# A conditioned LoRA kernel: tile 1 of x loaded behind W and transposed by VectorE, and the rounded part of M multiplied in front of its remainder

## The reference, cut to what matters

```python
# x (64, 32, 512): 64 samples of 32 rows; W0 (16, 32, 32); W (512, 512); A (5, 512, 32); Bw (512, 32)
x = x + einsum('bct,bcd->bdt', x, W0[cond])           # mix: each sample's 32 rows by its own 32x32 matrix
x = x + einsum('bsi,oi->bso', x, W)                    # base, the same for all samples
      + 0.5 * einsum('bsr,or->bso', einsum('bsi,bir->bsr', x, A[label]), Bw)
```

## Time and profile before

| | us |
|---|---|
| median of 3 runs | 75.79 (75.51, 75.79, 79.14) |
| the profiled execution, its own time | 74.88 |
| its span in the trace | 73.1 |
| PE busy | 69.3 |
| DVE busy | 41.7 |
| ACT busy | 34.9 |
| POOL busy | 32.2 |

### The profile page before, as it was taken

How to read it: one execution, slowest core, us unless ns; L and a number is a source line. 1 busy time by engine, 2 the same in 40 slices (tenths; PEclk the granted TensorE clock), 3 DMA queues, 4 the chain that set the end, 5 groups by cost and what they waited for, 6 DMA issues and landing times.

```text
span 73.1 us, 2439 instructions
## 1 busy us (share of the span) xinstructions
PE 69.3 (95%) x1006; PEld 55.7 (76%) x1006; DVE 41.7 (57%) x64; ACT 34.9 (48%) x83; POOL 32.2 (44%) x75
## 2 busy tenths in 40 slices
PE   4999999999999999999999999999999999999950
PEld 3788999987786768888687588888876788858930
DVE  4018769999489799919972669439016190213220
ACT  1536667699033974729702452834915538004100
POOL 4652678699980047878932058867000100000000
PEclk9999999999999999999999999999999999999999
DMA  0989999345397650048965000059910000599694
GB/s 7 328 259 372 226 238 205 63 134 151 101 211 263 182 127 13 9 95 196 283 174 158 9 4 17 19 137 181 247 36 9 0 0 0 117 192 264 186 241 158
DMA packets 11727, 10.25 MB, mean 140 GB/s; under 512 B 1092, under 2 KB 9028, under 8 KB 11716
## 3 DMA queue, kind: packets, MB, share of 16 engines
q1 hardware_dynamic: 11200, 9.83, 53.2%
q0 software_dynamic: 512, 0.26, 1.9%
q10 hardware_dynamic: 4, 0.00, 0.0%
HBM read 5.90 MB, written 4.19 MB: 138 GB/s over the span
## 4 chain that ended last, share of the span: by engine, by line
PE 95%; DVE 1%; issue 0%
PE p_u L642 18%; PE p_u L643 17%; PE p_u L644 17%; PE p_low L624 7%; PE p_y L653 5%; PE p_u L648 4%; PE p_low L709 4%; PE p_y L686 4%; PE p_fold L633 3%; PE p_y L642 3%; PE p_y L644 3%; PE p_y L643 3%; PE p_y L678 1%; PE p_low L695 1%; PE p_fold L695 1%; PE p_low L644 1%
## 5 line engine op out<-in xcount | busy, mean ns | idle before, releaser
L642 PE MATMUL p_u<-m_hi,xt_hi 128*128 128x512 f32 (+2 forms) x66 | 24.1, 364 | 0.0
L643 PE MATMUL p_u<-m_lo,xt_hi 128*128 128x512 f32 (+2 forms) x66 | 23.3, 354 | 0.0
L644 PE MATMUL p_u<-m_hi,xt_lo 128*128 128x512 f32 (+2 forms) x66 | 23.3, 354 | 0.0
L291 POOL DMA_INDIRECT w_sel<-in_L_cond_weights,w_row x16 | 16.9, 1057 | 12.3 <-PE p_y L653 8.0
L642 PEld LDWEIGHTS p_u<-m_hi,xt_hi 128*128 128x128 f32 x66 | 12.5, 189 | 2.2 <-issue 0.6
L644 PEld LDWEIGHTS p_u<-m_hi,xt_lo 128*128 128x128 f32 x66 | 12.5, 189 | 1.8
L643 PEld LDWEIGHTS p_u<-m_lo,xt_hi 128*128 128x128 f32 x66 | 12.5, 189 | 1.6
L469 DVE STREAM_TRANSPOSE xt<-x_sb 128x512 f32<-128x512 f32 x12 | 13.0, 1105 | 0.1
L498 DVE COPY u_sb<-p_u 128x512 f32<-128x512 f32 x6 | 4.2, 692 | 12.4 <-PE p_u L648 10.1
L370 ACT ACTIVATE xt_hi<-xt 128x512 fp32r<-128x512 f32 x12 | 6.9, 627 | 7.3 <-PE p_u L648 5.1
L492 DVE TENSOR_TENSOR xt_lo<-xt,xt_hi 128x512 fp32r<-128x512 f32 x12 | 8.4, 732 | 0.2
(11 more groups left out here) (80 smaller groups left out, 80.2 us busy)
## 6 DMA issues: line engine op xcount, KB each, us to landing
x_sb<-in_x SPq DMA_DIRECT2D x24, 128.0 KB
out<-y_sb SPq DMA_DIRECT2D x12, 256.0 KB
w_sb<-in_L_cond_W SPq DMA_DIRECT2D x4, 256.0 KB, 4.1
x_rows<-in_x SPq DMA_DIRECT2D x2, 256.0 KB, 3.5
x_rows<-in_x SPq DMA_DIRECT2D x1, 512.0 KB, 5.0
out<-y_two SPq DMA_DIRECT2D x4, 128.0 KB
a_sb<-in_L_cond_lora_A SPq DMA_DIRECT2D x1, 320.0 KB
w_sel<-in_L_cond_weights,w_row POOLq DMA_INDIRECT x16, 4.0
```

What stands on the lines that cost most here:

```text
L291: nc.gpsimd.indirect_dma_start(out=w0_sel[:, t, :], out_offset=None, in_=W0_rows, in_offset=bass.IndirectOffsetOnAxis(ap=w0_row[:, t:t + 1 ...
L642: mm(to, xt_hi[:, slot, c, rows], m_hi[:, c, cols], start=(c == 0 and first), stop=False)
L643: mm(to, xt_hi[:, slot, c, rows], m_lo[:, c, cols], start=False, stop=False)
L644: mm(to, xt_lo[:, slot, c, rows], m_hi[:, c, cols], start=False, stop=False)
```

## The change

SP loads all four blocks of W one behind the other. Tile 1 comes behind them, not as rows but as the second half of pair 0 in the layout of the pairs (four DMAs of 64 KB), in slot 0 of `x_sb`. DVE transposes it between the remainders of the third and the fourth block of M; ACT rounds it behind its fourth `split_m`; DVE subtracts. The second `transpose_rows`, `split_rows` and `keep_rows` are gone. Pair 2 uses the same slot, so its load waits for that transpose (`s_x1_t`). On PE the products of tile 0 with `m_hi` (eight matmuls a half) stand in front of those with `m_lo` (four a half), each half in 256 columns, and tile 1 is one `main_tile` of 512 columns.

```diff
             sp.dma_start(x_rows[:, 0], x_tile[0]).then_inc(s_rows_in[0], 16)
-            for o in W_ORDER[:2]:
+            for o in W_ORDER:
                 sp.dma_start(w_sb[:, o], W[P * o:P * (o + 1), :]).then_inc(s_w_in[o], 16)
-            sp.dma_start(x_rows[:, 1], x_tile[1]).then_inc(s_rows_in[1], 16)
-            for o in W_ORDER[2:]:
-                sp.dma_start(w_sb[:, o], W[P * o:P * (o + 1), :]).then_inc(s_w_in[o], 16)
+            for q in range(Q):
+                sp.dma_start(x_sb[R * q:R * (q + 1), 0, 1], x_pair[0, q][:, BT:2 * BT]).then_inc(s_x1_in, 16)
             sp.dma_start(bw_sb[:].rearrange("p o r -> p (o r)"), Bw_cols).then_inc(s_bw_in, 16)
             load(1, 1)
             sp.dma_start(a_sb[:].rearrange("p (l n) -> p l n", l=NL), A_cols).then_inc(s_a_in, 16)
+            sp.wait_ge(s_x1_t, 1)
             load(2, 0)
...
             split_m(1)
-            split_rows(1, p_fold)
             split_m(2)
             split_m(3)
+            act.wait_ge(s_x1_t, 1)
+            nc.scalar.activation(xt_hi[:, 0, :, P:2 * P], xt[:, 0, 1], COPY).then_inc(s_xhi, 1)
             keep_rows(0, p_low)
...
-            keep_rows(1, p_fold)
...
             split_m(1)
-            split_rows(1, p_fold)
             split_m(2)
+            dve.wait_ge(s_x1_in, 16 * Q)
+            nc.vector.transpose(xt[:, 0, 1].rearrange("p c (b s) -> p c b s", s=S),
+                                x_sb[:, 0, 1].rearrange("p b (i c) -> p c b i", c=C)).then_inc(s_x1_t, 1)
             split_m(3)
+            dve.wait_ge(s_x1_t, 1)
+            dve.wait_ge(s_xhi, 2)
+            nc.vector.tensor_tensor(xt_lo[:, 0, :, P:2 * P], xt[:, 0, 1], xt_hi[:, 0, :, P:2 * P].bitcast(F32),
+                                    ALU.subtract).then_inc(s_xlo, 1)
...
+            def main_rounded(bank, u, cols, first):
...
+                for c in range(C):
+                    mm(bank[:, cols], xt_hi[:, 0, c, rows], m_hi[:, c, cols], start=(c == 0 and first), stop=False)
+                for c in range(C):
+                    mm(bank[:, cols], xt_lo[:, 0, c, rows], m_hi[:, c, cols], start=False, stop=False)
+
+            def main_remainder(bank, u, cols):
...
+                for c in range(C):
+                    mm(bank[:, cols], xt_hi[:, 0, c, rows], m_lo[:, c, cols], start=False, stop=False)
...
             transpose_w(1)
-            transpose_rows(1, p_fold)
...
+            transpose_w(2)
+
+            pe.wait_ge(s_xlo, 1)
+            pe.wait_ge(s_mhi, 2)
+            main_rounded(p_u[0], 0, left, True)
             pe.wait_ge(s_diag_pool, 3)
             transpose_w(3)
...
+            pe.wait_ge(s_mlo, 2)
+            main_remainder(p_u[0], 0, left)
+            pe.wait_ge(s_mhi, 4)
+            main_rounded(p_u[0], 0, right, False)
+            pe.wait_ge(s_mlo, 4)
+            main_remainder(p_u[0], 0, right)
             pe.wait_ge(s_xlo, 2)
             pe.wait_ge(s_cond_sb, 1)
-            main_tile(p_u[1], 0, 1, left)
...
+            main_tile(p_u[1], 0, 1)
             transpose_b(p_y[0])
-            main_tile(p_u[1], 0, 1, right, first=False)
```

More of the change, by code:

```diff
@@ L129, in conditioned_lora_kernel @@
         s_w_in = [sem(f"s_w_in{i}") for i in range(OC)]
-        s_rows_in = [sem(f"s_rows_in{i}") for i in range(2)]
+        s_rows_in = [sem("s_rows_in0")]
+        s_x1_in = sem("s_x1_in")
+        s_x1_t = sem("s_x1_t")
         s_x_in = [sem(f"s_x_in{i}") for i in range(2)]
@@ L222, in _ @@
             load_next(4)
-            sp.wait_ge(s_rows_t, 2)
+            sp.wait_ge(s_rows_t, 1)
             sp.dma_start(x_rows[:], x_two[PAIRS - 1]).then_inc(s_last_in, 16)
@@ L615, in low_group @@
                         pe.wait_ge(s_a_act, HS * (k + 1))
-                    if t < 2:
-                        pe.wait_ge(s_rows_xt, t + 1)
+                    if t == 0:
+                        pe.wait_ge(s_rows_xt, 1)
+                    elif t == 1:
+                        pe.wait_ge(s_x1_t, 1)
                     elif t < LAST:
@@ L644, in main_tile @@
                     mm(to, xt_lo[:, slot, c, rows], m_hi[:, c, cols], start=False, stop=False)
+            def main_rounded(bank, u, cols, first):
+                rows = slice(P * u, P * (u + 1))
+                for c in range(C):
[3 more added lines that the diff above has]
+            def main_remainder(bank, u, cols):
+                rows = slice(P * u, P * (u + 1))
+                for c in range(C):
+                    mm(bank[:, cols], xt_hi[:, 0, c, rows], m_lo[:, c, cols], start=False, stop=False)
             def delta_tile(bank, u, cols=slice(0, O)):
@@ L719, in _ @@
             transpose_w(1)
-            transpose_rows(1, p_fold)
[L722 to L725, removed]
             pe.wait_ge(s_diag_pool, 2)
             transpose_w(2)
-            pe.wait_ge(s_mlo, 2)
-            main_tile(p_u[0], 0, 0, block[1], first=False, chunks=(0, 1))
+            pe.wait_ge(s_xlo, 1)
+            pe.wait_ge(s_mhi, 2)
+            main_rounded(p_u[0], 0, left, True)
             pe.wait_ge(s_diag_pool, 3)
             transpose_w(3)
-            main_tile(p_u[0], 0, 0, left, chunks=(2, 3))
+            pe.wait_ge(s_mlo, 2)
[4 more added lines that the diff above has]
+            main_remainder(p_u[0], 0, right)
             pe.wait_ge(s_xlo, 2)
             pe.wait_ge(s_cond_sb, 1)
-            main_tile(p_u[1], 0, 1, left)
-            pe.wait_ge(s_mlo, 4)
-            main_tile(p_u[0], 0, 0, right, first=False)
+            main_tile(p_u[1], 0, 1)
             transpose_b(p_y[0])
-            main_tile(p_u[1], 0, 1, right, first=False)
             pe.wait_ge(s_xlo, 3)
```

## The result

The changed kernel is slower: 79.02 us, the median of six runs (77.84 to 80.85), against 75.88 (75.21 to 79.14) for six of the kernel before. The ratio is 1.0439, 95% interval [1.0358, 1.0520]. The forecast was 75.9 with a range up to 77.2. A median is of all runs; a ratio compares the undisturbed executions of both kernels alone, since each of these kernels is some per cent slower in some of its executions.

What follows compares the result with a forecast made beforehand. The prediction took the start of dense work plus PE's work as the bound. It added -0.07 ahead of tile 2 and 0.25 behind it, about +0.2 us on 75.65, giving 75.9 us, range 74.6 to 77.2.

Steps and rivals of the forecast that it cites:

- The part ahead of tile 2: PE's start, up to tile 2's first matmul: forecast at 15.01 in place of 15.08, 0.07 us earlier.
- the four waits: PE idle four times between 6.6 and 11.9: 0.59, 0.5, 0.14 and 0.27 us, about 1.5 us together.
- The two for DVE: PE waits 0.14 us for the fourth m_lo, then 0.27 us for x_lo of tile 1, which starts at 11.9.
- the landing of tile 1's rows at 6.58: Rows there when PE reached them at 6.58; 6.6 taken as landing of W's third block in that slot.
- the forecast chain: From the third block's landing through POOL, PE, ACT and five pieces of DVE to tile 1 at 11.90.
- Behind it the same order runs with the same distances, so all moves by 0.2: Behind `copy_low`, where DVE becomes later than PE by 0.18 to 0.25 us: everything shifts by 0.2 us.
- The sum: Whole kernel: -0.07 ahead of tile 2 plus 0.25 behind it, about +0.2 us, giving 75.9 us.
- Saved work kept: Rival: PE's saved work stays saved, 0.6 to 1.33 us faster, 74.3 to 75.1 us; chance 0.13.
- Late loads: Rival: tile 1 or pair 1 lands after DVE asks (9.25, 11.75); 76.7 us at 1 us late; chance 0.17.
- The clock: Rival: holes in PE's work keep the clock low from 7.6 to 11.6, +2.0 us, 77.9; chance 0.08.
- PE's 1.33 us less of work: Dropped transposes 0.61, wider matmuls for tile 0 0.60 and tile 1 0.12, if PE never waited.
- DVE's 1.08 us more: DVE loses 0.69 and gains 1.08 + 0.69 us; the net 1.08 is all on its chain.

Runs made afterwards that it cites:

- e10: The changed kernel with six small unused matmuls (24 instructions) between tile 1 and `transpose_b`, tile 1 still in 512 columns; 76.34 us, ratio 1.0186.
- r_before: The kernel before, unchanged, run once more with a profile; 75.69 us over eleven runs, ratio 0.9986.
- r_after: The changed kernel, unchanged, run once more with a profile; 79.67 us.
- e3: The kernel before with only PE's new order of products; layout, loads and the other engines as before; 79.43 us, ratio 1.0586.
- e6: The changed kernel with SP holding back the loads of pair 4 and the last pair's rows until `low_group(1)` is done; 82.63 us, ratio 1.0970.
- e1: The changed kernel with 22 small unused matmuls on PE ahead of the first rounded half; 78.25 us, ratio 1.0274.
- e2: The changed kernel with tile 1 in a buffer of its own, so SP does not wait ahead of pair 2; 79.82 us, ratio 1.0615.
- e5: The changed kernel with tile 1 back in two halves of 256 columns, 24 more PE instructions; 76.94 us, ratio 1.0106.
- e7: The kernel before with 53 small unused matmuls (212 PE instructions) between tile 1 and tile 2; 80.88 us.
- e9: The kernel before with only PE's new order, and tile 1 in two halves of 256 columns (1000 pairs); 76.63 us, ratio 1.0146.
- e8: The changed kernel with tile 1 in halves of 256 columns and three unused 512-column matmuls in PE's holes; 76.45 us.

## Why the prediction was wrong

**The part ahead of tile 2 was about right.** Forecast 15.01, measured 14.64 in the changed kernel and 15.77 in e10 with 0.6 of pads. Of the four waits, 1.5 us by forecast, the changed kernel shows two, both ended by ACT's `m_hi`: 0.29 us of idle time ahead of 7.63 and 0.21 ahead of 10.00 (about 0.5 and 0.4 by the starts of the matmuls). The two for DVE did not come: tile 1 started at 11.54, straight behind tile 0, forecast 11.90. For POOL had the third block at 5.85, not 6.6. What I called the landing of tile 1's rows at 6.58 was only when PE came to them; the block in that slot was there 0.7 us sooner. In e10, where the third block came at 6.58, the forecast chain is there within 0.1 us: transpose of tile 1 at 9.25 (forecast 9.25), the fourth m_lo at 10.28 (10.35), x_lo at 11.13 (11.05), tile 1 at 11.88 (11.90). The 0.4 us won in the changed kernel was given back where forecast: DVE's L562 behind `transpose_b`, its transposes of pair 2 at 17.00 (forecast 17.37), `copy_low` at 19.25 without idle time (forecast 19.50). At `low_group(1)` the changed kernel stood at -0.08 us, forecast +0.2.

**The step that failed is "Behind it the same order runs with the same distances, so all moves by 0.2".** The order did not change there, but 44 instructions fewer stood ahead of it, and PE gets its program in pieces of 256. The sum had no term for the arrival of PE's own instructions, and neither did a rival. In the changed kernel it is 2.58 us of the 3.3 by which the span grew (and the last copy of DVE, at 73.11 against 70.38, is later by 2.73). The other 0.6 lie behind it: the last store ended 2.15 us behind its issue at 73.56, before 1.50 behind 70.83. Why is open.

**The rivals.** Saved work kept: no. Late loads: DVE did wait 0.66 us for pair 1 in e10, but lost nothing by it at `copy_low`, and in the changed kernel L471 shows no idle time at all ahead of pair 1. The clock: in the profile behind the result it did not fall. It did fall in both kernels when the second block of W was late (r_before, r_after), so it explains slower single runs of either and not the ratio. It also fell behind the stop of 2.08 us in e3 and the wait of 2.9 us in e6: a stop can cost more than its own length. I had called a hole of at most 0.6 us an argument against it; in e1 holes of 1.11 and 0.59 us came ahead of the fall, in r_before one of 1.95.

The Trainium skill (TensorE: Matmul & The Clock Gate, Part 1) has the clock fall back after an idle stretch. This case agrees in r_before: PE was idle for most of 6 to 8 us, then the granted clock read 0.50.

One reading of the earlier trace rows needs care: the windows read 1.00 also ahead of the first record of the clock, where the warm-up matmuls of 0.49 us each ran at the lower level. In e2, e3, e5, e7 and e9 that first record came only at 10.1 to 10.6 us, and matmuls of 128 or 256 columns lay 0.21 to 0.25 us apart until then, twice what they cost in the earlier trace rows. There the distance between matmuls tells the clock, and the window does not.

**What the change is worth without the stop.** e5 is at 1.0106 [0.9965, 1.0247] and e10 at 1.0186 [1.0145, 1.0228] of the kernel before. So even then no gain is shown. Of PE's 1.33 us less of work 0.44 were left at tile 2 of the changed kernel and 0.08 at `low_group(1)`: the rest became waits, and DVE's 1.08 us more is on the path through `copy_low`, as forecast. The two ratios are about +0.8 and +1.4 us; less what the added matmuls cost (0.1 by the earlier trace rows and 0.6 as measured) both leave about 0.7 or 0.8, an estimate, against +0.2 forecast. So the sum was some 0.5 us short besides. Later blocks of W make that much in the profile of e10; whether they do in its other runs is not shown. No kernel here beats the kernel before.

**What stays open.** Which event makes PE ask for its next piece. In the kernel before a piece moved between 20 and 22 us, in the changed one behind 24.8, though no more than 44 instructions lay between them; a rule by count alone failed in e7, and the request itself is in no row. What is shown is that in `low_group` PE uses up 128 pairs in 1.30 us, against 34 instructions in the 3.6 us of tile 3 and the deltas, and that it went on 2.45 us or more behind the start of the packet. So a packet that starts only when `low_group(1)` does comes too late even with the DMA engines empty (e6, 0.95 us of stop), and later still with them 99.7% busy.

The Trainium skill (Runtime: NRT & Kernel Launch, Instruction fetch mechanics) says that the program is refilled in blocks of 16 KiB, 256 instructions, fetched while the current one runs, and that the cost of crossing a border is mostly hidden. The block size agrees with q8's 8 packets and 0.13 MB here; "mostly hidden" does not, with 2.58 us at one border.

## What to carry to other kernels

An engine that works through thousands of short instructions can run out of its own program: a stop marked "issue" in the middle of a run of equal instructions, with the instruction queue's packet starting only 2.5 us or less ahead of its end, was that in all five profiles here that have it. Here 24 instructions more or fewer ahead of such a run brought the stop or took it away, so repeat a slower version with a few unused small matmuls added (six were enough here) before its idea is thrown away, and look at a fast one with the same suspicion. And an engine's saved work counts only up to the next engine on the path: here DVE took 1.08 us more where PE took 1.33 less, and 0.08 us were left.

## What had not been expected of the hardware

- 24 instructions more made the kernel about 2 to 3 us faster, twice (e5 against the changed kernel, e9 against e3) by splitting matmuls and once (e10) by work that is thrown away.
- PE went on 2.45 to 2.58 us behind the start of the packet with its next instructions in all five stops, while the packet itself took 1.0.
- Small float32 matmuls of 32 columns count as two pairs each (22 written, x44 in the trace; 53 written, x106). In `low_group` 128 pairs take 1.36 us; between other work 106 took 3.54 us and 44 at the lower clock 2.45.
- The arrival of the second block of W, counted by POOL's start on its diagonal, varied from 5.20 to 6.83 us between profiles, and the clock went with it. In the six profiles with 5.70 or less, e8 with its fillers among them, TensorE was at the higher level from 7.3 us on at the latest; in the eight with 5.88 or more it was at the lower one until some point between 10.1 and 11.2 us. That this makes much of the spread from 74.7 to 78 us of one and the same kernel is likely but not shown: only two runs of that kernel were profiled.
